# Wk and Wq loaded as fp32 on the sync queue and cast on VectorE and ScalarE; the key constants and the bv centring moved to later places

## The chip, the cores and the metric

The kernel runs as one program on all 8 cores of one Trainium2 chip. Each core computes two of the sixteen sequences and exchanges nothing with the others. The metric is the device time of the slowest core in microseconds, as a median over runs.

## What is computed

One transformer layer over X of 16 sequences, T = 2048 tokens, E = 1024 channels. The attention part, cut to what matters here (the softmax runs over the queries i, axis -2, and there is a residual with a layernorm behind it):

```python
q = einsum('bte,fe->btf', X, Wq) + bq
k = einsum('bte,fe->btf', X, Wk) + bk
v = einsum('bte,fe->btf', X, Wv) + bv
scores = where(j > i, -inf, einsum('bie,bje->bij', q, k) / sqrt(E))
x = layernorm(X + einsum('bij,bje->bie', softmax(scores, axis=-2), v))
```

Behind it stand three feed-forward blocks, each of two 1024 x 1024 linear layers whose weights are dequantized (q/7.5 - 1, times a scale per 16 columns) with a rank-32 addition (lora), a layernorm and a GELU between them, a residual around each block, and a last layernorm.

## The kernel before

**Engines and queues.** The program is written as five in-order lists, one for each engine (`pe`, `dve`, `act`, `pool`, `sp`). Each entry names the tokens it waits for, and it holds up everything behind it on its engine. `pool.dma` issues a transfer on GpSimd's queue, `sp.dma` one on SyncE's. A transfer may change the type only on GpSimd's.

**Order of the work on a core.** The scores need only the product B = Wk^T Wq, so the key and query projections are never formed.

- Constants: `cf` and `cb` are loaded on SyncE. VectorE writes a few memsets, one of them `ones_f` (token `k_of`). Two small fp32 matmuls on TensorE use them, and they are first in TensorE's list.
- BT: 128 matmuls of 128x512 in two halves h of 64 each (8 banks, the contraction index o outermost). The matmuls of o wait for `k_wk[o]` and `k_wq[h][o]`. Behind each half the 8 banks are evicted to bf16 by VectorE and ScalarE in turn.
- Small vectors: 2 x 64 matmuls of 128x2 (`small_vec`).
- `h_chunk` for the four X chunks of 512 tokens: 8 groups of 8 matmuls each, evicted by VectorE and ScalarE in turn. `v_chunk`: 8 groups, each evicted by VectorE with `BVC` (bv with its mean taken off) added, so each waits for `k_bvc`.
- `c_bias`: 32 matmuls of 32x512 that sum over X, then ScalarE copies the bank into `RS` (`tc`) and `SQ` (`th`), and then come 16 one-column fp32 matmuls that turn the row into columns (the key constants, `S_CJ`); every fourth one waits for the one before. The softmax's exponent uses them, the V groups don't.
- Scores and softmax by `s_row`, weighted sums by `pv_chunk`, then the feed-forward part.

In the first sequence the order is h_chunk 0 to 3, centring of Wv after chunk 2, centring of bv, `c_bias`, v_chunk 0 to 3. In the second it is h_chunk 0, then h_chunk and v_chunk in turn, `c_bias`, v_chunk 3; bv is loaded again after h_chunk 0, since its space was used in between.

**Work in the background.** The 48 pieces of dequantization (`dq_slot`) are placed in the lists every 39 units, where a group of 8 matmuls counts 8 units. A slot puts a ScalarE scaling that waits for the load of the integer weights (`qw_t`), a GpSimd product with the scales (`sc_t`), two lora matmuls on TensorE, two VectorE sums, for even layers a ScalarE cast, and the next two 512 KB loads on SyncE. A slot's scaling uses loads that the slot before it issued.

**PSUM.** 8 banks go round in a fixed ring: `bank_take` gives the one returned longest ago. A group whose bank has not been evicted waits.

**Loads at the start.** GpSimd's queue holds 8 loads of Wk rows and 16 of Wq half rows, all cast to bf16 on the way, then three X chunks, the lora parts and the last X chunk, all cast too. SyncE's list holds `cf`, `cb`, then Wv, bv and the first dequantization loads, all behind `k_x[1]`, the second X chunk.

Of the kernel before, what the change touches and what calls it, by code (L numbers as in the profile page):

```python
# [11 lines left out]
AF = mybir.ActivationFunctionType  # L12
# [6 lines left out]
EC = 8  # L19
# [8 lines left out]
A_H = 10240  # L28
A_V = 18432
# [97 lines left out]
def build_program():  # L127
# [4 lines left out]
    wq = din("wq", [E, E], F32)  # L132
    wk = din("wk", [E, E], F32)
    wv_t = din("wv_t", [E, E], F32)
    bv_h = din("bv_h", [128, E], F32)
# [11 lines left out]
    with ExitStack() as ctx:  # L147
# [14 lines left out]
        f32v = lambda a, n: plf[:, a:a + n]  # L162
# [13 lines left out]
        pe, dve, act, pool, sp = (Queue(newsem()) for _ in range(5))  # L176
        slot = lambda: Slot(newsem())
# [4 lines left out]
        def bank_take():  # L182
            return free.pop(0)
# [5 lines left out]
        groups = [0]  # L189
        units = [0.0]  # L190
# [4 lines left out]
        def after_groups(n, fn):  # L195
            due.append((groups[0] + n, fn))
            due.sort(key=lambda d: d[0])
# [35 lines left out]
        def v_stt(out, a, s, b, op0, op1, *after, acc=None, rev=False):  # L233
# [4 lines left out]
        s_cf, s_cb, s_bv = slot(), slot(), slot()  # L238
# [4 lines left out]
        WK = [b16v(A_R + o * 512, 1024) for o in range(EC)]  # L243
        WQ = [b16v(A_DQ + o * 512, 1024) for o in range(EC)]
        XT = [[b16v(A_XT + s * 2048 + c * 256, 512) for c in range(EC)] for s in range(4)]
        XT3 = [b16v(A_XT + s * 2048, 4096).rearrange("p (c t) -> p c t", t=TT)
               for s in range(4)]
        xsrc = [xt[s].rearrange("(c p) t -> p c t", p=128) for s in range(NSEQ)]
        k_wk, k_wq = [None] * EC, [[None] * EC, [None] * EC]
        for o in range(EC):  # L250
            k_wk[o] = pool.dma(slot(), WK[o], wk[o * 128:(o + 1) * 128, :])
            k_wq[0][o] = pool.dma(slot(), WQ[o][:, 0:512], wq[o * 128:(o + 1) * 128, 0:512])
        s_q1 = slot()
        for o in range(EC):
            k_wq[1][o] = pool.dma(slot() if o in (0, EC - 1) else s_q1, WQ[o][:, 512:1024],
                                  wq[o * 128:(o + 1) * 128, 512:1024])
        for o in range(1, EC - 1):
            k_wq[1][o] = (s_q1.sem, s_q1.n)
        s_x = [slot() for _ in range(4)]

        def load_x(seq, ic, s, *after):
            return pool.dma(s_x[s], XT3[s], xsrc[seq][:, :, ic * TT:(ic + 1) * TT], *after)
# [5 lines left out]
        def load_lora(first):  # L268
# [5 lines left out]
            for d in range(2):  # L274
                for dst, src in ((la, la_h[first:first + 2]),
# [2 lines left out]
                                       src.rearrange("w r e -> (w r) e"), *lora_free))  # L278
            k_lora[:] = ks

        k_x = [load_x(0, ic, ic) for ic in range(3)]
        load_lora(0)
        k_x.append(load_x(0, 3, 3))
        k_wv = [sp.dma(slot(), f32v(A_V + o * 1024, 1024), wv_t[o * 128:(o + 1) * 128, :],
                       k_x[1]) for o in range(EC)]
        k_bv = sp.dma(s_bv, f32v(A_BVC, 1024), bv_h, k_x[1])


# [37 lines left out]
        for h in range(2):  # L326
            bk = [bank_take() for _ in range(EC)]
            for o in range(EC):
                for et in range(EC):
# [4 lines left out]
                    if o == EC - 1:  # L334
                        dst, src = BT[et][:, h * 512:(h + 1) * 512], ps[bk[et][0]][:]
                        if et % 2:
                            t = a_act(dst, src, AF.Copy, p)
                        else:
                            t = dve.put(lambda e, d=dst, s=src: e.tensor_copy(d, s), p)
# [34 lines left out]
        BVC = f32v(A_BVC, 1024)  # L374

        def centre_wv():
            for c in range(EC):
                st = f32v(A_V + c * 1024, 1024)
                rs = col(S_ROW + c)
                t = a_act(st, st, AF.Copy, k_wv[c], acc=rs)  # L380
                t2 = v_ts1(col(S_ROW + 8 + c), rs, 1.0 / E, ALU.mult, t)
                k_wvc.append(v_ts1(WV[c], st, col(S_ROW + 8 + c), ALU.subtract, t2))

        def centre_bv(tok):
            t = a_act(BVC, BVC, AF.Copy, tok, acc=col(S_T + 26))
            t2 = v_ts1(col(S_T + 27), col(S_T + 26), 1.0 / E, ALU.mult, t)
            return v_ts1(BVC, BVC, col(S_T + 27), ALU.subtract, t2)
# [106 lines left out]
        sq_free = [None] * NSQ  # L494
# [11 lines left out]
        def h_chunk(seq, jc, xs):  # L506
            for ft in range(EC):
                b, fr = bank_take()
                for c in range(EC):
                    p = mm(ps[b][:], BT[c][:, ft * 128:(ft + 1) * 128], XT[xs][c],  # L510
                           c == 0, c == EC - 1, k_bt[c][ft // 4], k_x[jc],
                           *(fr if c == 0 else ()), sig=c == EC - 1)
                dst = Hb[:, 4 * jc:4 * jc + 4, ft, :]
                src = ps[b][:].rearrange("p (j t) -> p j t", t=128)
                if ft % 2:
                    t = a_act(dst, src, AF.Identity, p, k_u, bias=col(S_U + ft), scale=1.0 / 32)
                else:
                    t = v_ts(dst, src, 1.0 / 32, col(S_U + ft), ALU.mult, ALU.add, p, k_u)
                k_h[jc].append(t)
                p_hlast[0] = p  # L520
                bank_give(b, t)
                group_end(8)
# [16 lines left out]
        def c_bias(seq, slots):  # L539


            b, fr = bank_take()
            b2, fr2 = bank_take()
            for c in range(EC):
                for jc in range(4):
                    g = 32 * jc
                    p = mm(ps[b][g:g + 32, :], hl[:, 32 + 32 * c:64 + 32 * c], XT[slots[jc]][c],
                           c == 0, c == EC - 1, k_w, k_x[jc], *fr, sig=c == EC - 1)
            tc = a_act(RS, ps[b][:], AF.Copy, p, *rs_free)
            th = a_act(SQ[0], ps[b][:], AF.Copy, p, sq_free[0])  # L550
            tl = v_tt(SQ[1], ps[b][:], SQ[0], ALU.subtract, th, tc, sq_free[1])
            bank_give(b, tl)
            for i, tok in enumerate((th, tl)):
                a = 2 * A_SQ + 512 * i
                k_mean[i] = sp.dma(s_mean[i], means[seq, :, i], plb[1:98:32, a:a + 512], tok)
                sq_free[i] = k_mean[i]
            rows = None
            for jt in range(16):
                g = 32 * (jt // 4)
                p = mm(ps[b2][:, jt:jt + 1],  # L560
                       RS[g:g + 1, (jt % 4) * 128:(jt % 4 + 1) * 128],
                       sm[g:g + 1, S_ONE:S_ONE + 1], True, True, tc, k_one, rows, *fr2,
                       sig=jt % 4 == 3)
                if jt % 4 == 3:
                    rows = p
            rs_free[:] = [p]

            t = v_ts(sm[:, S_T + 40:S_T + 56], ps[b2][:, 0:16], float(E), col(S_T + 24),
                     ALU.mult, ALU.add, p, k_bqbk)
            bank_give(b2, t)  # L570
            k_cj[0] = v_ts1(sm[:, S_CJ:S_CJ + 16], sm[:, S_T + 40:S_T + 56], 1.0 / 32, ALU.mult, t)
            groups[0] += 2
            units[0] += 12

        def load_mr(seq, ic):

# [238 lines left out]
        for seq in range(NSEQ):  # L815
            sl = slots[seq]
            k_h = [[] for _ in range(4)]
            k_v = [None] * 16
            if seq == 0:
                for jc in range(4):  # L820
                    h_chunk(seq, jc, sl[jc])
                    if jc == 2:
                        centre_wv()
                k_bvc = centre_bv(k_bv)
                c_bias(seq, sl)
                load_r(0, 0)
                load_r(0, 1)
                for ic in range(4):
                    v_chunk(seq, ic, sl[ic])
            else:  # L830
                for ic in range(4):
                    h_chunk(seq, ic, sl[ic])
                    if ic > 0:
                        v_chunk(seq, ic - 1, sl[ic - 1])
                    if ic == 0:

                        k_bvc = centre_bv(sp.dma(s_bv, BVC, bv_h, *sq_free))
                        load_r(1, 0)
                    if ic == 2:
                        while pieces:  # L840
                            pieces.pop(0)()
                        load_r(1, 1)
                c_bias(seq, sl)
                v_chunk(seq, 3, sl[3])
            k_x_next = [None] * 4
            prev = None
            load_mr(seq, 0)
            load_mr(seq, 1)
            for ic in range(4):
                if ic == 3 and seq == 1:  # L850
                    ffn_prefetch()
                for jt in (range(0, 6), range(6, 10), range(10, 16), ())[ic]:
                    row = s_row(jt, sl)
                    if prev is not None:
                        z_row(prev)
                    prev = row
                    if seq == 0 and jt % 4 == 3:
                        k_x_next[jt // 4] = load_x(1, jt // 4, jt // 4, xt_read[jt // 4])
                if ic == 2:
                    z_row(prev)  # L860
                pv_chunk(seq, ic)
            if seq == 0:
                k_x = k_x_next
# [330 lines left out]
```

How the kernel before makes its waits and increments, by code:

```python
    def emit(self, e, last):  # L108
        for todo, fn, sem, by in self.items:
            for s, v in todo:
                e.wait_ge(s, v)
            inst = fn(e)
            if sem is not None:
                inst.then_inc(sem, by)
        for s, v in last:
            e.wait_ge(s, v)
```

## Time and profile before

| what | value |
|---|---|
| median of 3 runs | 1403.29 us (1401.22 to 1404.46) |
| profiled execution, its own time | 1395.1 us |
| its span on the slowest core (core 2) | 1393.5 us |
| spans of the eight cores | 1381.3 to 1393.5 us |
| TensorE busy, share of the span | 1300.7 us, 93% |
| ScalarE, VectorE, GpSimd busy | 746.1, 704.3, 356.1 us |
| mean granted TensorE clock, by core | 0.975 to 0.981 |
| HBM read, written | 158.85, 46.15 MB |

The profiled execution is 8 us shorter than the median of the unprofiled runs; sums over its rows are made against 1395.1 us and carried over to the median as a difference. Rows name instructions by the tensors they touch: POOLT is the one large SBUF tensor in which X, the weights and all intermediate tiles lie; CF, CB, SM and HL are small constants and statistics; ps are the PSUM banks. A transfer that casts is counted by the bytes that it writes. "Idle before" is the time for which the engine did nothing just ahead of a row, with the event that ended it.

### The profile page before, as it was taken

Reading aid. Unit: us, or ns where it says so; the run is one execution under the profiler, and the core shown is the slowest. Engines: PE = TensorE matmul, PEld = TensorE weight load, DVE = VectorE, ACT = ScalarE, POOL = GpSimd, SP = SyncE. Lnnn points to the kernel's source line nnn. Section 1 sums busy time; section 2 is a strip of 40 time slices with the busy share of each in tenths; the row PEclk is TensorE's granted clock in tenths of the full one; section 3 lists DMA queues with packets and bytes.
Section 4 is the critical chain, followed back from the end, with each engine's and each line's share of the span. In section 5 each row is a group of like instructions: output and inputs, shape, how many; then the busy total and the mean of one; then the engine's idle time right before and its main releaser. Section 6 shows DMA issues by size and latency. Waiting matters only on the chain.

```text
span 1393.5 us, 21058 instructions; the slowest of 8 cores (1381.3 to 1393.5 us)
## 1 busy us (share of the span) xinstructions
PE 1300.7 (93%) x6611; PEld 611.1 (44%) x6740; DVE 704.3 (51%) x1487; ACT 746.1 (54%) x1100; POOL 356.1 (26%) x284
## 2 busy tenths in 40 slices
PE   5997999898899999999999999999899999999994
PEld 2444444443344444444444444455444444444552
DVE  1133556543344456446553483677435534736774
ACT  0153226663223276536855884776578558748641
POOL 5022333565543225332000075001100000840010
PEclk9998999999999999999999999999999999999997
DMA  9956546796856345692101055025801010640032
GB/s 136 208 187 208 178 142 165 216 254 234 295 146 212 114 152 186 216 364 87 61 1 61 1 198 165 0 98 206 287 16 61 1 61 20 207 137 1 31 121 91
DMA packets 71371, 192.61 MB, mean 138 GB/s; under 512 B 6032, under 2 KB 16864, under 8 KB 68192
## 3 DMA queue, kind: packets, MB, share of 16 engines
q1 hardware_dynamic: 48352, 133.45, 29.1%
q0 software_dynamic: 22912, 57.81, 15.2%
q8 instruction: 57, 0.93, 0.3%
q14 instruction: 50, 0.41, 0.1%
HBM read 158.85 MB, written 46.15 MB: 147 GB/s over the span
## 4 chain that ended last, share of the span: by engine, by line
PE 72%; DMA 10%; DVE 6%; issue 4%; ACT 4%; POOL 2%; SPq 1%; DVEq 0%; ACTq 0%; POOLq 0%
PE ps L217 72%; ACT POOLT L221 4%; DMA POOLT<-qw_t 3%; DMA POOLT<-xt 2%; DMA x1s<-POOLT 2%; DVE POOLT L225 2%; DVE SM L1032 1%; POOL POOLT L105 1%; DVE SM L234 1%; DMA POOLT<-bv_h 1%; SPq L105 1%; DMA POOLT<-sc_t 1%; DMA POOLT<-lb_h 1%; POOL POOLT L684 1%; DVEq L111 0%
## 5 line engine op out<-in xcount | busy, mean ns | idle before, releaser
L217 PE MATMUL ps<-POOLT 128*128 128x512 bf16 (+3 forms) x5476 | 1225.2, 375 | 37.1 <-DMA POOLT<-wq 11.5
L217 PEld LDWEIGHTS ps<-POOLT 128*128 128x128 bf16 x5600 | 532.9, 98 | 664.5 <-issue 91.7
L221 ACT ACTIVATE POOLT<-ps,SM 128x512 bf16<-128x512 f32 (+4 forms) x396 | 262.2, 682 | 249.3 <-PE ps L217 152.2
L225 DVE TENSOR_TENSOR POOLT<-POOLT 128x512 bf16<-128x512 bf16 (+1 forms) x448 | 256.4, 608 | 209.5 <-ACT POOLT L221 187.0
L221 ACT ACTIVATE POOLT<-POOLT 128x512 bf16<-128x512 f32 (+4 forms) x234 | 175.3, 762 | 225.1 <-DMA POOLT<-qw_t 108.1
L225 DVE TENSOR_TENSOR POOLT<-ps,POOLT 128x512 bf16<-128x512 f32 (+1 forms) x186 | 124.2, 688 | 151.9 <-PE ps L217 126.9
L990 POOL TENSOR_TENSOR POOLT<-POOLT 128x512 f32<-128x512 f32 x64 | 89.6, 1424 | 371.1 <-DMA POOLT<-x1s 361.9
L411 POOL TENSOR_TENSOR POOLT<-POOLT 128x1024 f32<-128x1024 f32 x48 | 112.7, 2348 | 263.1 <-DMA POOLT<-sc_t 169.6
L221 ACT ACTIVATE POOLT<-POOLT,CF 128x512 bf16<-128x512 bf16 x192 | 154.3, 808 | 27.5 <-DVE POOLT L225 26.5
L221 ACT ACTIVATE POOLT<-POOLT,SM 128x512 bf16<-128x512 f32 (+2 forms) x120 | 109.8, 917 | 83.3 <-DVE SM L228 47.8
L234 DVE SCALAR_TENSOR_TENSOR POOLT<-ps,SM,POOLT 128x512 f32<-128x512 f32 x128 | 96.1, 750 | 80.8 <-PE ps L217 80.3
L217 PE MATMUL ps<-POOLT,CB 128*128 128x512 bf16 (+2 forms) x331 | 96.8, 383 | 24.5 <-ACT POOLT L221 13.4
L684 POOL TENSOR_TENSOR POOLT<-POOLT 128x1024 f32<-128x1024 f32 x32 | 75.0, 2362 | 54.7 <-ACT POOLT L221 53.5
L221 ACT ACT_TABLE_LOAD x48 | 61.6, 1283 | 34.8 <-PE ps L217 30.7
L105 POOL DMA_DIRECT2D out<-POOLT x28 | 15.0, 535 | 252.0 <-ACT POOLT L221 252.0
L600 DVE TENSOR_REDUCE SM<-ps 128x1 f32<-128x512 f32 (+3 forms) x80 | 48.9, 611 | 39.7 <-PE ps L217 36.4
L217 PEld LDWEIGHTS ps<-POOLT,CB 128*128 128x128 bf16 (+2 forms) x336 | 25.6, 96 | 66.0 <-issue 45.8
L228 DVE TENSOR_SCALAR POOLT<-ps,SM 128x512 bf16<-128x512 f32 (+1 forms) x36 | 26.9, 755 | 45.8 <-PE ps L217 45.0
L1032 DVE BATCH_NORM_STATS2 SM<-ps 128x6 f32<-128x512 f32 x64 | 43.4, 692 | 10.9 <-PE ps L217 9.0
L217 PEld LDWEIGHTS ps<-CB,POOLT 128*128 128x128 bf16 x512 | 34.4, 99 | 15.4 <-issue 0.6
L217 PE MATMUL ps<-CB,POOLT 128*128 128x128 bf16 x512 | 39.5, 221 | 0.0
L105 POOL DMA_DIRECT2D weffs<-POOLT x48 | 28.6, 597 | 41.8 <-ACT POOLT L221 33.4
(53 smaller groups left out, 250.7 us busy)
## 6 DMA issues: line engine op xcount, KB each, us to landing
POOLT<-qw_t SPq DMA_DIRECT2D x48, 512.0 KB, 4.0
POOLT<-sc_t SPq DMA_DIRECT2D x48, 512.0 KB, 5.5
POOLT<-weffs SPq DMA_DIRECT2D x24, 1024.0 KB, 7.8
POOLT<-xt SPq DMA_DIRECT2D x16, 1024.0 KB, 10.5
x1s<-POOLT POOLq DMA_DIRECT2D x16, 1024.0 KB, 9.2
POOLT<-x1s SPq DMA_DIRECT2D x8, 2048.0 KB, 11.8
POOLT<-x1s SPq DMA_DIRECT2D x64, 256.0 KB, 3.1
out<-POOLT POOLq DMA_DIRECT2D x28, 512.0 KB, 3.8
```

Source lines behind the costliest of these rows:

```text
L105: self.items.append((todo, lambda e: e.dma_start(out=out, in_=in_), slot.sem, 16))
L217: return pe.put(lambda e: e.matmul(out, lhsT, rhs, start=start, stop=stop), *after, sig=sig)
L221: return act.put(lambda e: e.activation(out, in_, func, bias=bias, scale=scale, accum_out=acc), *after)
L225: return dve.put(lambda e: e.tensor_tensor(out, a, b, op), *after)
L228: return dve.put(lambda e: e.tensor_scalar(out, a, s1, s2, op0, op1), *after)
L234: return dve.put(lambda e: e.scalar_tensor_tensor(out, a, s, b, op0, op1, accum_out=acc, reverse1=rev), *after)
L411: dq_ab[s] = pool.put(lambda e: e.tensor_tensor(q, q, f32v(a + 1024, 1024), ALU.mult), t, dq_ld[s][1])
L600: t = dve.put(lambda e, b=b, lo=lo, n=n: e.tensor_reduce(col(ro + n), ps[b][:, lo:512], AX.X, ALU.max, negate=True), p)
L684: ta = pool.put(lambda e: e.tensor_tensor(r3, r3, rb, ALU.mult), t, *k_r)
L990: tr = pool.put(lambda e, h=h, q=q: e.tensor_tensor(h, h, FXR[q], ALU.add), kx, hb[o], th)
L1032: tb.append(dve.put(lambda e, b=b, k2=k2, fo=fo: e.bn_stats(sm[:, fo + 6 * k2:fo + 6 * k2 + 6], ps[b][:]), p, *fin_free[i]))
```

## The change

Four edits are made together.

1. Wk and Wq are loaded as fp32 on SyncE's queue into staging space (Wk where H will lie, Wq where Wv's staging lies). VectorE casts each Wk block to bf16 (`load_k`), ScalarE each Wq half block (`load_q`).
2. The first three X loads, still on GpSimd's queue with a cast, wait for `q_ld[1][5]`, the load of the 22nd of the 24 weight blocks. Each Wv load waits for the cast that frees its staging space as well.
3. In `c_bias` the 16 one-column matmuls and the two VectorE operations behind them go to a function of their own, `c_columns`, which runs 6 groups later, among the V groups.
4. bv: in the first sequence it is centred behind `c_bias` and not ahead of it. In the second it is loaded at the same place as before, and centred after h_chunk 1 and not after h_chunk 0.

```diff
+        def load_q(h, o):
+            dst = f32v(A_V + o * 1024 + h * 512, 512)
+            q_ld[h][o] = sp.dma(slot(), dst, wq[o * 128:(o + 1) * 128, h * 512:(h + 1) * 512])
+            k_wq[h][o] = act.put(lambda e: e.activation(
+                WQ[o][:, h * 512:(h + 1) * 512], dst, AF.Copy, bias=0.0, scale=1.0), q_ld[h][o])
+
+        def load_k(o):
+            dst = f32v(A_H + o * 1024, 1024)
+            t = sp.dma(slot(), dst, wk[o * 128:(o + 1) * 128, :])
+            k_wk[o] = dve.put(lambda e: e.tensor_copy(WK[o], dst), t)
+
         for o in range(EC):
-            k_wk[o] = pool.dma(slot(), WK[o], wk[o * 128:(o + 1) * 128, :])
-            k_wq[0][o] = pool.dma(slot(), WQ[o][:, 0:512], wq[o * 128:(o + 1) * 128, 0:512])
...
+            load_k(o)
+            load_q(0, o)
         for o in range(EC):
...
+            load_q(1, o)
...
-        k_x = [load_x(0, ic, ic) for ic in range(3)]
+        k_x = [load_x(0, ic, ic, q_ld[1][5]) for ic in range(3)]
...
-                       k_x[1]) for o in range(EC)]
+                       k_x[1], k_wq[1][o]) for o in range(EC)]
...
+            groups[0] += 2
+            units[0] += 12
+            after_groups(6, lambda: c_columns(tc))
+
+        def c_columns(tc):
+            b2, fr2 = bank_take()
             rows = None
             for jt in range(16):
...
+                c_bias(seq, sl)
                 k_bvc = centre_bv(k_bv)
-                c_bias(seq, sl)
...
                 for ic in range(4):
                     h_chunk(seq, ic, sl[ic])
+                    if ic == 1:
+                        k_bvc = centre_bv(k_bv)
                     if ic > 0:
                         v_chunk(seq, ic - 1, sl[ic - 1])
                     if ic == 0:
 
-                        k_bvc = centre_bv(sp.dma(s_bv, BVC, bv_h, *sq_free))
+                        k_bv = sp.dma(s_bv, BVC, bv_h, *sq_free)
                         load_r(1, 0)
```

The head of VectorE's list (the eight casts are those of Wk; L299 writes `ones_f`, for which TensorE's first matmul waits):

```order
-L1139 UNCONDITIONAL_BRANCH
-L289 MEMSET POOLT 128x128
-L290 MEMSET SM 128x1
-L291 MEMSET SM 128x1
-L292 MEMSET HL 128x256
+L1154 UNCONDITIONAL_BRANCH
+L262 CAST POOLT<-POOLT 128x1024 x8
+L299 MEMSET POOLT 128x128
+L300 MEMSET SM 128x1
+L301 MEMSET SM 128x1
+L302 MEMSET HL 128x256
 L231 TENSOR_SCALAR HL<-CF 128x16
```

The casts stand ahead of the memsets, because the list is filled in the order in which the code is written and `load_k` is called first.

TensorE's list around `c_bias` of the first sequence (the 264 are the four h_chunks with 8 lora matmuls, the 32 are `c_bias`, the 16 of one column are the key constants):

```order
 L217 MATMUL ps<-POOLT 128x512 x264
 L217 MATMUL ps<-POOLT,HL 32x512 x32
+L217 MATMUL ps<-POOLT 128x512 x50
 L217 MATMUL ps<-SM,POOLT 128x1 x16
-L217 MATMUL ps<-POOLT 128x512 x278
+L217 MATMUL ps<-POOLT 128x512 x228
```

Six V groups (48 matmuls) and one slot's two lora matmuls now stand between `c_bias` and the columns. The second sequence shows the same move.

ScalarE's list around the second centring of bv (128x4x128 are evictions of h_chunk groups, the plain 128x1024 are the scalings of the dequantization, which wait for `qw_t`; the one that also writes SM is the centring's sum):

```order
 L221 ACTIVATE POOLT<-ps,SM 128x4x128 x2
 L221 ACTIVATE POOLT<-POOLT 128x1024
-L221 ACTIVATE POOLT<-ps,SM 128x4x128
+L221 ACTIVATE POOLT<-ps,SM 128x4x128 x3
+L221 ACTIVATE POOLT<-POOLT 128x1024
+L221 ACTIVATE POOLT<-ps,SM 128x4x128 x2
+L221 ACTIVATE POOLT<-POOLT 128x1024
 L221 ACTIVATE POOLT,SM<-POOLT 128x1024
-L221 ACTIVATE POOLT<-ps,SM 128x4x128 x2
-L221 ACTIVATE POOLT<-POOLT 128x1024
-L221 ACTIVATE POOLT<-ps,SM 128x4x128 x2
-L221 ACTIVATE POOLT<-POOLT 128x1024 x2
```

The centring has moved behind all four evictions that ScalarE makes of h_chunk 1 and behind two more scalings, the second of which stands right ahead of it.

## Rows read from the trace of the kernel before

**Rows 1.** The page: busy times, and the chain that ended last, by engine

```profile
PE 1300.7 (93%) x6611; PEld 611.1 (44%) x6740; DVE 704.3 (51%) x1487; ACT 746.1 (54%) x1100; POOL 356.1 (26%) x284
...
PE 72%; DMA 10%; DVE 6%; issue 4%; ACT 4%; POOL 2%; SPq 1%; DVEq 0%; ACTq 0%; POOLq 0%
```

**Rows 2.** Timeline of TensorE, core 2: start, duration, ..., [idle before, what ended it]

```profile
3.39 0.63 PE L217 MATMUL ps<-CF,POOLT 128*128 128x48 f32 x2 [3.39 <-DMA CF<-cf_h]
9.17 5.83 PE L217 MATMUL ps<-POOLT 128*128 128x512 bf16 x16 [4.67 <-DMA POOLT<-wq]
...
35.85 12.25 PE L217 MATMUL ps<-POOLT 128*128 128x512 bf16 x55 [2.08 <-DMA POOLT<-wq]
51.47 31.30 PE L217 MATMUL ps<-POOLT 128*128 128x512 bf16 x135 [0.19 <-issue]
83.56 23.46 PE L217 MATMUL ps<-POOLT 128*128 128x512 bf16 x106 [0.80 <-ACT POOLT L221]
```

**Rows 3.** Busy time by stretch, core 2; last three: granted clock, DMA share, GB/s

```profile
10.00:15.00 5.00, 4.99 (x15) 1.65 (x13) 0.00 (x0) 0.00 (x0) 5.00 (x10) 1.00 1.05 129
...
30.00:35.00 5.00, 3.16 (x14) 1.06 (x11) 2.18 (x4) 3.24 (x5) 0.00 (x0) 1.00 1.17 172
...
50.00:55.00 5.00, 4.81 (x62) 2.57 (x60) 0.76 (x4) 0.00 (x0) 0.00 (x0) 0.66 1.11 171
...
70.00:75.00 5.00, 4.95 (x24) 2.25 (x23) 0.75 (x1) 0.69 (x1) 0.00 (x0) 1.00 1.01 302
```

**Rows 4.** Waits of SyncE's queue: total us, times, longest

```profile
SPq L111 <- DMA POOLT<-xt: 47.9, 1, 47.9
```

**Rows 5.** Timeline of VectorE at the start, and its casts by shape

```profile
1.16 0.17 DVE L289 MEMSET POOLT<- 128x128 f32 x1 [1.16 <-PEq L128]
3.71 0.08 DVE L298 DVE_READ_ACCUMULATOR SM<-CF 128x1 f32 x1
...
L764 DVE CAST POOLT<-POOLT 128x2048 bf16<-128x2048 f32 x8 | 9.4, 1220 | 0.0
```

**Rows 6.** Timeline around c_bias of the first sequence

```profile
112.48 1.91 PE L217 MATMUL ps<-POOLT,HL 128*32 128x512 bf16 x32
115.48 1.06 ACT L221 ACTIVATE POOLT<-POOLT 128x1024 f32<-128x1024 int32 x1 [3.81 <-DMA POOLT<-qw_t]
119.08 1.07 ACT L221 ACTIVATE POOLT<-ps 128x512 f32<-128x512 f32 x2
119.81 7.77 PE L217 MATMUL ps<-SM,POOLT 1*128 1x1 f32 x32 [5.42 <-ACT POOLT L221]
127.91 13.55 PE L217 MATMUL ps<-POOLT 128*128 128x512 bf16 x51 [0.33 <-issue]
```

**Rows 7.** Busy time by stretch behind that c_bias, columns as in Rows 3

```profile
118.00:120.00 2.00, 0.19 (x1) 0.22 (x2) 0.61 (x2) 2.00 (x5) 2.00 (x2) 0.87 0.60 145
...
132.00:134.00 2.00, 2.00 (x8) 0.83 (x7) 1.34 (x5) 0.41 (x1) 0.00 (x0) 0.71 1.00 316
```

**Rows 8.** Timeline and one stretch around the second bv load

```profile
369.51 1.06 ACT L221 ACTIVATE POOLT<-POOLT 128x1024 f32<-128x1024 f32 x1 [11.18 <-DMA POOLT<-bv_h]
...
372.78 12.48 PE L217 MATMUL ps<-POOLT 128*128 128x512 bf16 x50 [4.44 <-DVE POOLT L228]
...
374.00:376.00 2.00, 2.00 (x7) 0.78 (x6) 1.15 (x2) 0.00 (x0) 1.86 (x2) 0.63 1.01 415
```

**Rows 9.** Timeline and one stretch around c_bias of the second sequence

```profile
455.11 2.19 PE L217 MATMUL ps<-SM,POOLT 1*128 1x1 f32 x16 [1.26 <-ACT POOLT L221]
457.44 3.81 PE L217 MATMUL ps<-SM,POOLT 1*128 1x1 f32 x16
461.59 17.65 PE L217 MATMUL ps<-POOLT 128*128 128x512 bf16 x74 [0.33 <-issue]
...
464.00:466.00 2.00, 2.00 (x10) 0.91 (x9) 0.69 (x1) 0.00 (x0) 0.00 (x0) 0.94 0.00 0
```

**Rows 10.** The same columns on core 6, timeline

```profile
455.36 4.77 PE L217 MATMUL ps<-SM,POOLT 1*128 1x1 f32 x32 [1.26 <-ACT POOLT L221]
```

More of the change, by code:

```diff
@@ L249, in build_program @@
         k_wk, k_wq = [None] * EC, [[None] * EC, [None] * EC]
+        q_ld = [[None] * EC, [None] * EC]
+        def load_q(h, o):
[7 more added lines that the diff above has]
+            k_wk[o] = dve.put(lambda e: e.tensor_copy(WK[o], dst), t)
         for o in range(EC):
-            k_wk[o] = pool.dma(slot(), WK[o], wk[o * 128:(o + 1) * 128, :])
-            k_wq[0][o] = pool.dma(slot(), WQ[o][:, 0:512], wq[o * 128:(o + 1) * 128, 0:512])
-        s_q1 = slot()
+            load_k(o)
+            load_q(0, o)
         for o in range(EC):
[L255 to L258, printed above, removed]
+            load_q(1, o)
         s_x = [slot() for _ in range(4)]
@@ L542, in c_bias @@
             b, fr = bank_take()
-            b2, fr2 = bank_take()
             for c in range(EC):
@@ L571, in c_bias @@
             k_cj[0] = v_ts1(sm[:, S_CJ:S_CJ + 16], sm[:, S_T + 40:S_T + 56], 1.0 / 32, ALU.mult, t)
-            groups[0] += 2
-            units[0] += 12
         def load_mr(seq, ic):
```

## The prediction

> **What bounds the kernel now.** I read the page first: TensorE is busy for 93% of the span and makes 72% of the chain that ended last [rows 1]. So an edit is worth what it takes from TensorE's list: gaps, work, or time at the lower clock. I then went through the timeline of TensorE alone for gaps, and looked only at the three places that the change touches. At the start TensorE waits for weights: its first large group begins at 9.17, the last wait of this kind ends at 35.85, and the H groups begin at 51.47 [rows 2]. Around the first `c_bias` it stands idle for 5.42 us, then runs the one-column matmuls for 7.77 us, then goes on at half clock [rows 6, 7]. Around the second bv load it stands for 4.44 us [rows 8], and around the second `c_bias` for 1.26 us [rows 9]. Everything behind moves with TensorE, so I add up these four places on core 2, the slowest.
>
> **The start: a loss.** Before, TensorE needs only Wk[0] and half of Wq[0] to begin, and works on while the rest lands. Now its very first matmul waits for `ones_f`, and VectorE writes that behind all eight casts of Wk. So the BT stage can't begin until Wk[7] has landed, although by then nearly all other weights are there. What is queued behind this wait is TensorE's whole list.
>
> When does Wk[7] land? Ahead of it, itself included, stand eight Wk blocks of 0.524 MB and seven half blocks of 0.262 MB: 6.03 MB. The first transfer (cf) ended TensorE's wait at 3.39 [rows 2]. For the rate I take 302 GB/s, the stretch in which fp32 loads of 4 KB rows from SyncE's queue ran with the transfer engines full [rows 3]: 6.03/0.302 = 20.0 us, so 23.4 us. Half blocks queued behind will get some share, since the sixteen engines don't run in step; an estimate of 1.5 us puts it at about 25 us. The bounds of the rate are the casting loads of before, counted by their fp32 source: 129 GB/s written is 258 read, 172 is 344 [rows 3]. They give 26.8 and 20.9 us, and with the same allowance at most 28.5.
>
> From there, step by step. The cast of 128x1024: the row of twice the size takes 1.22 us [rows 5]; less an assumed fixed 0.15 us, half of it is 0.7. Then VectorE's small operations: from 1.16 to 3.79, less the wait for cf inside, 1.0 us [rows 5], and the second small matmul 0.55; the old wait for Wq began at 9.17 - 4.67 = 4.50, which fits [rows 2]. BT begins near 27.3. Its 128 matmuls, now without a wait: 56 took 12.25 us (one record is missing), 0.219 each, so 28.0. The first 16 took 5.83 and not 3.5, as the clock starts low, 2.3 more [rows 2]. I add 0.2 for the banks between the halves: 30.5 us, ending near 57.8. The second halves of Wq, 8.39 MB in all, are there by 3.4 + 27.8 = 31 and needed from 42 on; ScalarE's sixteen casts end by 33, ahead of its first eviction. Then the small vectors: 51.47 - (35.85 + 12.25) = 3.4 us. The H groups begin at 61.2 and not at 51.47: **a loss of 9.7 us**, 5.6 to 13.2 by the bounds.
>
> The X loads wait behind the weights, but the first is cast and landed well before 61: from 29 us on, 2.1 MB of source at these rates is 7 us. SyncE was held until about 50 by the second X chunk (47.9 us of wait [rows 4]); that chunk now lands at about the same time, so Wv and the first dequantization loads do too. TensorE comes 9.7 us later to them, so the 0.80 us gap before 83.56 [rows 2], where ScalarE waited for `qw_t` with evictions behind it, should go: **0.8 us gained**. GpSimd loses 24 issues ahead of X; nothing waits for them.
>
> A rule of the Trainium skill speaks against hoping for more from the new queue: "DMA: Bandwidth & Descriptors", section "Issuing engines are not separate DMA queues", says that transfers issued by any engine run on the same 16 engines, and that another issuer saves only issue time. By it the weights land no sooner than the bytes allow; the rows agree (DMA share 1.05 to 1.17 with GpSimd's queue [rows 3]).
>
> **The first c_bias.** Its matmuls end at 112.48 + 1.91 = 114.39. ScalarE stood for `qw_t` until 115.48 and had a last H eviction and bv's centring to do before the two copies at 119.08. The columns ran from 119.81, and V began at 127.91: 13.5 us [rows 6]. The clock row of 0.87 puts the fall to the lower level at 119.5, and the row of 0.71 the rise at 133.2 [rows 7]. V thus ran 5.25 us at half speed and lost 2.6. Together **16.1 us**. Now V follows `c_bias` at once. Its evictions wait for `k_bvc`, some 2.5 us behind the copies, near 121.5 on the old time. By then three or four V groups, `c_bias` and the last H group hold banks of the ring of eight, so TensorE doesn't stop. The columns remain as work. At the full clock they take 4.77 us [rows 10]; on core 2 the clock fell within them (2.19 us for the first half, 3.81 for the second [rows 9]). Bounds: 4.8 with nothing behind, and 7.77 + 0.33 + 2.6 = 10.7 when all is as slow as before. Now busy V groups stand ahead of them and no idle stretch, so I take a value near the fast end: 4.8 + 0.3, and 1.3 for a fall that comes late, 6.4. **Gain 9.7 us** (5.4 to 11.3).
>
> The skill's page "TensorE: Matmul & The Clock Gate", section "What's actually happening", says that the throttled clock is the default and that activity releases it. By this the columns, which keep the array nearly empty, still bring a fall; with the full slow price the sum would be 4.3 us worse at each place.
>
> **The second c_bias.** It ends at 455.11 - 1.26 = 453.85 and V begins at 461.59: 7.7 us. The row of 0.94 puts the clock's rise at 464.2 [rows 9], so V lost 1.3 more: 9.0 us. Less the same 6.4: **gain 2.6 us** (-1.7 to 4.2).
>
> **The second bv.** ScalarE waited 11.18 us for bv, with H evictions behind it, and TensorE 4.44 us for a bank. The row of 0.63 puts the clock's rise at 375.5, so 2.7 us from 372.78 at half speed cost 1.35 more [rows 8]. Now bv, which landed at 369.5, is asked for after h_chunk 1, near 372. **Gain 5.8 us** (0 if a new wait takes its place, see below).
>
> **Sum.** 9.7 + 2.6 + 5.8 + 0.8 = 18.9 gained, 9.7 lost: 9.2 us less, 1395.1 to 1385.9 for the profiled execution. The median of the runs shown is 1403.3, so 1394.1.
>
> **Rivals.**
>
> Loads faster than I take. At 344 GB/s without drift Wk[7] lands at 20.9, the start costs 5.6 and the net is -13.3; with the columns at their fast end at both places -16.5, so 1387 to 1390. For it speaks the 172 row; against it that it stood in one stretch only. The skill's first page above, section "Anatomy of one DMA", fits 436 GB/s behind a fixed 2 us; by that Wk[7] would land near 17 and the net would be -17. The one row above 400 GB/s is a stretch of 2 us (415 [rows 8]); stretches of 5 us stay at 302 or below, by fp32 source at 344.
>
> The gap by bv returns elsewhere. A scaling that waits for `qw_t` now stands right ahead of the centring [the order above shows it]. Its load is issued when bv and two X halves are under way, and TensorE is there 5.8 us earlier. If it lands 8 us or more behind h_chunk 1, V groups fill the ring of banks and TensorE stops again: up to 5.8 us come back. That alone makes the net -3.4; slow columns at both places alone (8.6 us) make it -0.6; both +5.2. So 1400, 1403 or 1408.5. Against it: eight banks are a cover of some 12 us of V groups.
>
> The start swallows it all, and the kernel is slower. The mechanism is the gate on Wk[7] alone: if the transfer engines serve the 24 weight blocks side by side, Wk[7] lands when all 8.39 MB have: at 302 GB/s at 31.2, a loss of 15.9 and a net of -3.0; at 258 GB/s at 35.9, a loss of 20.6 and a net of +1.7. It decides from 34 us on; from 37 us on the kernel is slower by over 0.2%, 1407 us or so. For it speaks that the half blocks are short rows; against it, that one queue serves its transfers roughly in the order of issue.
>
> That the change does nothing is hard to hold: the gate on `ones_f` and the moved columns are both in the lists.
>
> **Chances and range.** My forecast, net -5 to -13, 1390 to 1398: 0.50. Faster loads: 0.14. A gap that returns or slow columns: 0.18. A start that swallows most or all: 0.18, half of it beyond zero net. 1386 to 1404 leaves out the ends of the last two. A measurement of this kernel tells 0.2%, some 2.8 us, from no change. Faster by over 0.2%: 0.74 (the first two, and a little over half of the third). Within 0.2%: 0.14. Slower: 0.12 (the start beyond 37 us, or both parts of the third).
>
> **What would show it.** In the profile after: the one wait of TensorE at the start ended by VectorE's memset near 26 us and BT without gaps behind; H groups from about 61; no idle time between `c_bias` and V in either sequence; the columns as one row of 5 to 6 us among V groups; no 4 us gap near 370. I am wrong if H begins past 70, if a wait on bank evictions shows in the V groups, or if the clock is low for over 4 us around the columns.

## The result, and the profile after

The change makes the kernel slower: 1408.66 us in the median of six runs against 1403.55 of the kernel before, a ratio of 1.0038 [1.002, 1.0056], some 5.3 us. The profiled execution took 1409.76 us. Its span is that of core 6 (1408.2), and cores 4 to 7 have a lower granted clock in it (0.968 to 0.971) than cores 0 to 3 (0.976 to 0.982), which those of before didn't show. So I read the change on core 2, which the prediction used: 1393.5 before, 1398.0 after. Executions in which some cores ran long stretches at a lower granted clock are left out of every ratio and mean core, but for one experiment where I say so; the medians in us beside them are taken over all executions.

The page, slowest core: busy times and the chain that ended last, as in [rows 1].

```profile
PE 1307.5 (93%) x6611; PEld 609.7 (43%) x6740; DVE 711.2 (51%) x1495; ACT 758.3 (54%) x1116; POOL 342.3 (24%) x260
...
PE 77%; DMA 7%; DVE 6%; issue 4%; ACT 3%; SPq 1%; POOL 1%; DVEq 0%; ACTq 0%; POOLq 0%
```

VectorE has 8 more instructions and ScalarE 16 (the casts), GpSimd 24 fewer (the issues). The share of waits for transfers in the chain fell from 10% to 7% [rows 1], and the kernel is slower all the same.

TensorE's timeline at the start, core 2, to be held against [rows 2]:

```profile
26.90 0.63 PE L217 MATMUL ps<-CF,POOLT 128*128 128x48 f32 x2 [26.90 <-DVE SM L301]
27.59 0.56 PE L217 MATMUL ps<-SM,POOLT 128*128 128x1 f32 x2
28.01 30.68 PE L217 MATMUL ps<-POOLT 128*128 128x512 bf16 x128
58.53 3.39 PE L217 MATMUL ps<-HL,POOLT 128*128 128x2 bf16 x128
61.78 3.40 PE L217 MATMUL ps<-POOLT 128*128 128x512 bf16 x9
```

VectorE's, with the first and the last of the eight casts of Wk, and two stretches of 5 us (granted clock, DMA share, GB/s at the end):

```profile
7.95 0.69 DVE L262 CAST POOLT<-POOLT 128x1024 bf16<-128x1024 f32 x1 [7.95 <-DMA POOLT<-wk]
...
25.92 0.69 DVE L262 CAST POOLT<-POOLT 128x1024 bf16<-128x1024 f32 x1 [1.26 <-DMA POOLT<-wk]
26.59 0.17 DVE L299 MEMSET POOLT<- 128x128 f32 x1
```

```profile
10.00:15.00 5.00, 0.00 (x0) 0.00 (x0) 1.07 (x2) 1.44 (x3) 0.00 (x0) 1.00 0.95 287
15.00:20.00 5.00, 0.00 (x0) 0.00 (x0) 1.70 (x3) 1.68 (x3) 0.00 (x0) 1.00 1.03 343
```

There is one wait of 26.9 us where there were several: `ones_f` is written at 26.59, behind the cast of Wk[7], and TensorE's first matmul follows it. Then the BT stage runs without a gap. Its first matmuls start 0.43 us apart and those behind 34 us 0.216, as at the start of BT before (16 matmuls in 5.83 us [rows 2]). The granted clock says 1.00 in both stretches all the same, so at the very start that column doesn't show what TensorE ran at:

```profile
28.00:32.00 4.00, 4.00 (x11) 1.47 (x12) 1.40 (x8) 2.53 (x5) 0.00 (x0) 1.00 0.94 320
36.00:40.00 4.00, 4.00 (x20) 1.85 (x19) 0.00 (x0) 0.00 (x0) 3.03 (x6) 1.00 1.01 115
```

Around the first `c_bias`, TensorE, core 2, and four stretches:

```profile
121.78 1.91 PE L217 MATMUL ps<-POOLT,HL 128*32 128x512 bf16 x32
123.62 10.96 PE L217 MATMUL ps<-POOLT 128*128 128x512 bf16 x50
134.51 1.05 PE L217 MATMUL ps<-SM,POOLT 1*128 1x1 f32 x8
135.71 2.19 PE L217 MATMUL ps<-SM,POOLT 1*128 1x1 f32 x16
...
138.59 0.47 PE L217 MATMUL ps<-SM,POOLT 1*128 1x1 f32 x3
138.99 21.28 PE L217 MATMUL ps<-POOLT 128*128 128x512 bf16 x90
```

```profile
139.00:140.00 1.00, 1.00 (x5) 0.45 (x5) 0.72 (x3) 0.00 (x0) 0.00 (x0) 0.77 0.90 348
140.00:142.00 2.00, 2.00 (x6) 0.71 (x5) 1.20 (x5) 0.00 (x0) 0.00 (x0) 0.50 1.04 339
142.00:144.00 2.00, 2.00 (x9) 0.81 (x8) 0.69 (x1) 0.00 (x0) 0.00 (x0) 0.76 0.98 341
144.00:146.00 2.00, 2.00 (x11) 0.91 (x10) 0.69 (x1) 0.00 (x0) 0.00 (x0) 1.00 1.09 335
```

V now follows at once; the 5.42 us of idle time of [rows 6] are gone. The columns take 4.55 us (134.51 to 139.06) and run at the full clock, but the clock falls to its lower level behind them, at 139.5, and rises at 143.0: 3.4 us of V groups at half speed, 1.7 us lost. In the second sequence the clock falls within the columns:

```profile
455.26 1.91 PE L217 MATMUL ps<-POOLT,HL 128*32 128x512 bf16 x32
457.10 10.96 PE L217 MATMUL ps<-POOLT 128*128 128x512 bf16 x50
467.99 5.93 PE L217 MATMUL ps<-SM,POOLT 1*128 1x1 f32 x32
473.86 7.54 PE L217 MATMUL ps<-POOLT 128*128 128x512 bf16 x26
```

Around the second bv, one view after the other: the timelines of TensorE, SyncE's queue, ScalarE and VectorE, and two stretches, all of core 2.

```profile
364.70 21.52 PE L217 MATMUL ps<-POOLT 128*128 128x512 bf16 x99
390.35 27.73 PE L217 MATMUL ps<-POOLT 128*128 128x512 bf16 x116 [4.13 <-DVE POOLT L225]
```

```profile
361.69 0.33 SPq L105 DMA_DIRECT2D POOLT<-bv_h  x1
362.11 1.32 SPq L105 DMA_DIRECT2D POOLT<-xt  x2
369.59 0.34 SPq L105 DMA_DIRECT2D POOLT<-qw_t  x1
```

```profile
375.10 0.69 ACT L221 ACTIVATE POOLT<-ps,SM 128x512 bf16<-128x512 f32 x1 [2.77 <-PE ps L217]
385.13 2.00 ACT L221 ACTIVATE POOLT<-POOLT 128x1024 f32<-128x1024 int32 x2 [9.35 <-DMA POOLT<-qw_t]
```

```profile
387.59 1.81 DVE L231 TENSOR_SCALAR POOLT<-POOLT,SM 128x1024 f32<-128x1024 f32 x1
389.51 5.47 DVE L225 TENSOR_TENSOR POOLT<-ps,POOLT 128x512 bf16<-128x512 f32 x9
```

```profile
390.00:392.00 2.00, 1.65 (x4) 0.59 (x5) 2.00 (x5) 0.00 (x0) 1.91 (x1) 0.50 0.34 131
392.00:394.00 2.00, 2.00 (x6) 0.76 (x5) 2.00 (x4) 0.00 (x0) 0.00 (x0) 0.50 0.00 0
```

The gap of [rows 8] near 370 is gone, and another stands at 386.2 to 390.35, in the V groups. ScalarE waited 9.35 us for `qw_t`; the second of the two activations grouped in the row at 385.13 is bv's centring. The load was issued at 369.59, behind bv and two X halves of 1 MB, and landed at 385.1, 15.5 us later. V's evictions (L225) wait for the centring (L231 ends it), so all eight banks were full, and behind the gap the clock is at its lower level. All eight cores show this gap, 3.93 to 7.86 us long and 5.6 in the mean; before, six cores had one of 2.38 to 4.44 near 370, and the mean over all eight was 2.8.

The first of each kind of operation, read from the traces as a mean over the eight cores, gives the balance by stage (after less before, us; a minus is earlier):

| up to | after | loads alone | columns alone | bv alone |
|---|---|---|---|---|
| first H eviction | +10.3 | +9.8 | -0.2 | +0.7 |
| last H eviction | +8.8 | +8.2 | +0.3 | +0.9 |
| first score row | +1.3 | +8.8 | -7.1 | +0.8 |
| H of sequence 2 begins | +2.2 | +8.3 | -8.6 | -1.3 |
| its third chunk | +5.8 | +8.1 | -9.3 | +1.2 |
| score rows of sequence 2 | +3.9 | +7.9 | -10.7 | +1.8 |
| end | +10.8 | +8.1 | -8.7 | +2.3 |

Over cores 0 to 3 alone the changed kernel ends at +4.7; what cores 4 to 7 lose behind the last score rows is taken up in the last section. Single stages between these points differ by 1 to 2 us from trace to trace.

### The profile page after: what moved, and what is told of

It is laid out like the page before. It is cut to its first block, busy times and chain, and to the rows that moved or that the text cites. A ratio compares the mean times of both kernels' runs of the same rounds, so it can differ in the third digit from the quotient of the medians.

```text
span 1408.2 us, 21109 instructions; the slowest of 8 cores (1388.6 to 1408.2 us)
## 1 busy us (share of the span) xinstructions
PE 1307.5 (93%) x6611; PEld 609.7 (43%) x6740; DVE 711.2 (51%) x1495; ACT 758.3 (54%) x1116; POOL 342.3 (24%) x260
## 4 chain that ended last, share of the span: by engine, by line
PE 77%; DMA 7%; DVE 6%; issue 4%; ACT 3%; SPq 1%; POOL 1%; DVEq 0%; ACTq 0%; POOLq 0%
PE ps L217 77%; ACT POOLT L221 3%; DMA x1s<-POOLT 3%; DMA POOLT<-qw_t 2%; DVE POOLT L225 2%; DVE SM L1047 1%; DMA POOLT<-wk 1%; DVE SM L234 1%; SPq L105 1%; DMA POOLT<-sc_t 1%; DMA POOLT<-lb_h 1%; DVE POOLT L231 1%; POOL POOLT L697 1%; DVEq L111 0%; DVE SM L225 0%
## 5 line engine op out<-in xcount | busy, mean ns | idle before, releaser
L225 DVE TENSOR_TENSOR POOLT<-POOLT 128x512 bf16<-128x512 bf16 (+1 forms) x448 | 255.8, 606 | 214.4 <-ACT POOLT L221 191.2
L225 DVE TENSOR_TENSOR POOLT<-ps,POOLT 128x512 bf16<-128x512 f32 (+1 forms) x186 | 123.1, 687 | 149.8 <-PE ps L217 114.9
L217 PEld LDWEIGHTS ps<-CB,POOLT 128*128 128x128 bf16 x512 | 34.0, 98 | 15.1
L234 DVE SCALAR_TENSOR_TENSOR POOLT<-POOLT,ps 128x512 f32<-128x512 f32 x48 | 30.9, 681 | 12.6 <-POOL POOLT L421 8.6
## 6 DMA issues: line engine op xcount, KB each, us to landing
POOLT<-x1s SPq DMA_DIRECT2D x8, 2048.0 KB, 12.8
```

The lines of the kernel that those rows point to most:

```text
L217: return pe.put(lambda e: e.matmul(out, lhsT, rhs, start=start, stop=stop), *after, sig=sig)
L225: return dve.put(lambda e: e.tensor_tensor(out, a, b, op), *after)
L234: return dve.put(lambda e: e.scalar_tensor_tensor(out, a, s, b, op0, op1, accum_out=acc, reverse1=rev), *after)
```

## The experiments

Each comparison is with the kernel before on the same chip. "Mean core" is the mean of the eight cores' spans over the executions that are compared, less the same of the kernel before.

### The loads alone

The kernel before with edits 1 and 2 only (the first two pieces of the diff).

> The kernel before with the new loads alone (Wk and Wq as fp32 on SyncE's queue, casts on VectorE and ScalarE, X behind them); columns and bv as before. My theory (the gate on Wk[7] costs what the sum said, and nothing gives it back): the H groups begin some 9 to 10 us later than in the kernel before, as they do in the changed kernel (65.1 against 54.8 on core 2), the gap around c_bias stays, and the total is 8 to 11 us over the kernel before. Rival (later waits for loads absorb the delay): H late by 9 to 10 us, but the total within 3 us of the kernel before.

Measured: 1410.03 against 1398.68 us, ratio 1.0067 [1.0042, 1.0091]; mean core +10.0. The first matmul of core 2 starts at 26.86 and H at 61.34. The loads are the loss, of the size forecast, and nothing gives it back: by the table it is 9.8 us at the first H eviction and still 8.1 at the end.

### The columns alone

Edit 3 only.

> The kernel before with the key constants turned six groups behind, and nothing else. Theory: the first gap goes, V follows c_bias at once, some 9 us gained by the first score row on core 2, 1 to 2 us more in the second sequence: 7 to 11 us faster in total. Rival (the gain is taken back by waits for transfers in the first sequence's weighted sums, as 3 to 4 us went there in the changed kernel): 4 to 7 us faster, with the loss between the first and the last weighted sum of the first sequence.

Measured: 1393.03 us, ratio 0.994 [0.9915, 0.9965]; mean core -8.4. Of this 7.1 us come by the first score row, and the weighted sums take nothing back, as the rival had it.

### The second centring alone

Edit 4 in the second sequence only:

```diff
                     h_chunk(seq, ic, sl[ic])
+                    if ic == 1:
+                        k_bvc = centre_bv(k_bv)
...
-                        k_bvc = centre_bv(sp.dma(s_bv, BVC, bv_h, *sq_free))
+                        k_bv = sp.dma(s_bv, BVC, bv_h, *sq_free)
```

> The kernel before with bv of the second sequence centred after h_chunk 1, and nothing else. Theory (a scaling that waits for its integer weights stands ahead of the centring, and that load comes late behind other transfers): a gap of 3 to 5 us returns among the first V groups, total within 2 us of the kernel before. Rival (the forecast): no gap near 370, 4 to 6 us faster.

Measured: 1399.63 us, ratio 1.0 [0.9985, 1.0016]; mean core +2.7. TensorE's timeline, and how long the `qw_t` loads between 340 and 390 took from issue to landing, core 2:

```profile
388.80 13.45 PE L217 MATMUL ps<-POOLT 128*128 128x512 bf16 x54 [5.54 <-DVE POOLT L225]
```

```profile
DMA to landing us min/median/max: 4.8/6.9/16.9
```

The new gap is there without the other edits. It costs all that the old one did, and 2.7 us more in the mean core. By mean cores the three sum to 10.0 - 8.4 + 2.7 = +4.3, and the changed kernel, run again below, has +4.8: there is no large interaction. Edit 4 in the first sequence has no run of its own; it is only in the runs that combine edits.

### Centring ahead of the scaling instead

The kernel before with bv loaded at its place and centred seven groups into h_chunk 1 (`late_centre` does what `k_bvc = centre_bv(k_bv)` did), so that no scaling with a late load stands right ahead of it:

```diff
-                        k_bvc = centre_bv(sp.dma(s_bv, BVC, bv_h, *sq_free))
+                        k_bv = sp.dma(s_bv, BVC, bv_h, *sq_free)
+                        after_groups(7, late_centre)
```

> The kernel before with bv of the second sequence centred after 7 of the 8 groups of h_chunk 1: one group earlier than in the change, so that in ScalarE's list it stands ahead of the scaling that waits for its weights. Theory (the scaling ahead of it made the new gap): no gap of over 1 us in h_chunk 1 or the V groups behind it, 3 to 6 us faster than the kernel before by the third H chunk of the second sequence. Rival (bv itself, or the ring of banks, is what is late, and any later place gives a gap): a gap stays, and the total is within 2 us of the kernel before.

Measured: 1393.16 against 1397.19 us, ratio 0.9945 [0.9922, 0.9968]; mean core -4.4. On core 2 that `qw_t` load is as late as before (16.1 us) and ScalarE waits 9.98 us for it, but neither the centring nor an eviction stands behind it; TensorE has one unbroken row, and no core has a gap of over 1 us there:

```profile
342.07 68.17 PE L217 MATMUL ps<-POOLT 128*128 128x512 bf16 x308
```

### The X halves later

Why did that `qw_t` load take 17 us, when the three before it took 4.8 to 6.9? The run with the bv edit alone, and the two X halves of sequence 2 issued behind v_chunk 0:

```diff
                         k_bv = sp.dma(s_bv, BVC, bv_h, *sq_free)
+                    if ic == 1:
                         load_r(1, 0)
```

> The kernel before with the second bv centred after h_chunk 1, and the two X halves of load_r(1, 0) issued behind v_chunk 0 and not behind bv. Theory (the qw_t load that the scaling waits for is late, because 2 MB of X halves stand in the transfer engines ahead of it): it lands some 7 us sooner than the 17 us of the run with the bv edit alone, TensorE's gap of 5.54 us near 388 goes or falls under 1 us, and the kernel comes out 3 to 6 us faster than before, ratio 0.996 to 0.998. Rival (the stores of x1s alone make it late, or a centring that simply stands too far back): gap of 3 us or more remains, ratio 0.999 to 1.003.

Measured: 1392.11 against 1397.87 us, ratio 0.9965 [0.995, 0.998]; mean core -3.3. The same two views as for the bv edit alone:

```profile
359.76 42.45 PE L217 MATMUL ps<-POOLT 128*128 128x512 bf16 x196
```

```profile
DMA to landing us min/median/max: 3.8/4.7/6.0
```

The centring stands where the change put it, the longest landing fell from 16.9 to 6.0 us, and the gap is gone on all eight cores. So the lateness came from the 2 MB of X ahead of the load, and with it out of the way the forecast gain of edit 4 is real. By the Trainium skill, "DMA: Bandwidth & Descriptors", section "Issuing engines are not separate DMA queues", transfers of all issuers run on the same 16 engines. The two runs don't test that, since bv, X and `qw_t` are all issued by SyncE: they show that a load is late by what the same issuer has under way ahead of it. GpSimd's stores are in both.

### The gate on Wk[7] taken away

The changed kernel with the memsets and the two small matmuls written ahead of the loads, so that they stand ahead of the casts in VectorE's list (the memset of `ones_f` stands here for the block that moves):

```diff
+        k_of = dve.put(lambda e: e.memset(ones_f, 1.0 / E))
...
         k_wk, k_wq = [None] * EC, [[None] * EC, [None] * EC]
...
-        k_of = dve.put(lambda e: e.memset(ones_f, 1.0 / E))
```

> The changed kernel with the block of small constants (memsets and what hangs on them) written ahead of the loads, so that VectorE does it before the eight casts and TensorE's first matmul waits for no cast. Theory: BT begins near 9 us, H near 47 and not 65; but ScalarE then comes early to the first scaling, whose integer weights land near 80, so that TensorE stops there for 4 to 6 us; in total 8 to 13 us faster than the changed kernel, which is 3 to 8 us faster than the kernel before. Rival (the weights on SyncE's queue land no earlier, block by block, than on GpSimd's): H near 52, and the total 8 us faster than the changed kernel.

Measured: 1392.63 against 1398.68 us, ratio 0.9954 [0.9937, 0.9972]; mean core -3.7. ScalarE's and TensorE's timeline, core 2:

```profile
30.13 4.46 ACT L291 ACTIVATE POOLT<-POOLT 128x512 bf16<-128x512 f32 x7 [1.12 <-DMA POOLT<-wq]
34.50 2.04 ACT L221 ACTIVATE POOLT<-ps 128x512 bf16<-128x512 f32 x4
```

```profile
12.13 13.07 PE L217 MATMUL ps<-POOLT 128*128 128x512 bf16 x48 [7.74 <-ACT POOLT L291]
...
35.22 16.70 PE L217 MATMUL ps<-POOLT 128*128 128x512 bf16 x63 [5.14 <-ACT POOLT L221]
```

In the mean core this is 8.5 us faster than the changed kernel (+4.8, run again below), the low end of what I expected and just as well the rival's 8; the places are neither's. BT begins at 12.13 on core 2 and not at 9.17: Wq[0] lands at 10.06, and ScalarE's table load (1.28 us) and cast (0.63) follow. On that block the rival is right: SyncE's queue brings it no sooner than GpSimd's did. H (after the row at 35.22 and the small vectors) begins only at 55, and so the stop expected near 80 doesn't come. The cast load has a second price, which the gate had hidden: ScalarE's casts of Wq's second halves stand ahead of its four evictions of BT's first half, and TensorE waits 5.14 us for them, then runs on at the lower clock (0.50 in the stretch from 35 to 40).

### Both mended, and a version that keeps the old loads

Two combinations. The first keeps the fp32 loads, with the gate taken away, the casts of Wq's second halves placed behind the first half's evictions and shared by VectorE and ScalarE, Wv's loads written behind them, and bv centred as seven groups into h_chunk 1. The second keeps the old loads and has the columns six groups behind, the first centring behind `c_bias`, and the same centring of the second bv.

> The same with the new loads kept, but mended twice: the small constants are done ahead of the casts, and the casts of Wq's second halves stand behind the evictions of the first BT half, four on each of VectorE and ScalarE. Theory (the new queue brings the weights no sooner; all that the loads cost was order in the lists): H begins at 50 to 52, level with the kernel before, and the total is within 2 us of the kernel with the old loads and the other two edits. Rival (loads on SyncE's queue cost by themselves, by X that comes later): 4 us or more slower than that kernel.

> The changed kernel with the old loads (cast on GpSimd's queue) and with the second bv centred one group earlier: columns six groups behind, bv of the first sequence behind c_bias. Theory: the gains of the columns (8.4) and of the bv place (3 to 6) add up, 11 to 14 us faster than the kernel before. Rival (waits for transfers take back what TensorE gains earlier): 6 to 10 us faster.

Measured on one chip, before 1397.19 us. Mended loads: 1398.95 us (1389.4 over the three executions compared), ratio 0.9932 [0.9907, 0.9957], mean core -8.0. Old loads: 1384.96 us, ratio 0.9902 [0.9879, 0.9924], mean core -11.2, over three as well, where the single edits sum to -8.4 - 4.4 = -12.8. With mended loads the first H eviction comes 1.4 us earlier than before in the mean over the cores, and the last 4.5 us later (old loads: 0.8 later both). On core 2 TensorE stands in the H stage behind a scaling, and SyncE comes to Wv, with the dequantization loads behind it, at 52.39, where it came at 49.90 in the kernel before (second row), since it waits for the second X chunk:

```profile
85.36 25.96 PE L217 MATMUL ps<-POOLT 128*128 128x512 bf16 x106 [4.56 <-ACT POOLT L221]
```

```profile
52.39 4.35 SPq L105 DMA_DIRECT2D POOLT<-wv_t  x8
```

```profile
49.90 4.97 SPq L105 DMA_DIRECT2D POOLT<-wv_t  x8
```

So here too the fp32 loads are worth nothing: what the start gains, the wait for `qw_t` takes, in part because TensorE is there earlier and in part because X, and with it `qw_t`, lands later, which is the rival's mechanism. The difference between the two lies between my "within 2 us" and the rival's "4 us or more" (3.2 us in the mean core, 4.5 between the medians of the executions compared), and their intervals overlap.

### The best version again, with and without the later X halves

> The same program as the fastest so far, for the comparison on one chip: 11 to 14 us faster than before, ratio 0.990 to 0.992.

> The fastest version so far (old loads, columns six groups behind, bv centred a chunk part ahead) with the same later X halves. Theory: bv and the scalings have no gap there any more, so the later load has nothing to give: within 1.5 us of the same version without it on this chip. Rival (the crowd of transfers also costs elsewhere): 2 us or more faster.

Measured, before 1397.87 us: 1382.82, ratio 0.9903 [0.9885, 0.9921], and with the later X halves 1382.29, ratio 0.9901 [0.9884, 0.9918]. The version beats the kernel before by 1% on both chips, and the changed kernel by more, and the X halves matter only while a scaling that V waits for stands behind them.

### The changed kernel again

> The changed kernel again, on the chip of the other experiments. Theory (the edits add up: loads +10, columns -8.4, the second bv +2.7 in the mean over the cores): 3 to 6 us slower than the kernel before, as far on one die as on the other. Rival (something of the whole change, not of its parts, costs more, as the 10 us by which cores 4 to 7 were behind in its profile): 8 us slower or more.

Measured: 1417.88 against 1397.19 us, ratio 1.01 [1.0059, 1.0141]. This ratio isn't one of the edits alone: in four of the seven executions that are compared, at least one pair of cores had a lower mean granted clock (about 0.96), and these took 1415.1 to 1420.9 us. The three without it took 1401.5 to 1403.5, some 5 us over the kernel before, mean core +4.8, as expected. Such a pair stands in 8 of all 11 executions of the changed kernel and in none of the 16 of the kernel before on this chip, but also in one of 5 and two of 6 of the two combinations. So the change may well bring it on; which edit does isn't settled. See the last section.

## Why the prediction was wrong

I forecast -9.2 us, and +5.3 was measured. Two of the three signs that I had named for being wrong came true: a wait on evictions in the V groups, and in the second sequence a clock that was low for over 4 us around the columns (6.8 us, from about 470.6 to 477.4). By the steps of the prediction:

- **The start: a loss of 9.7.** Right. BT began at 28.0 on core 2 (forecast 27.3), H at 61.8 (61.2), the first H eviction 10.3 us late on core 2 and in the mean; with the loads alone it is 9.8 in the mean. The rate of 302 GB/s that I took lies between those of the two stretches (287 and 343). The rivals "loads faster" and "the start swallows it all" are out: the casts show the weights landing in order, Wk[7] at 25.9. The 436 GB/s that the prediction took from the Trainium skill is a fit for transfers that GpSimd issues; these are SyncE's, and no stretch of 5 us of them moved more than 343.
- **0.8 us in the H stage.** Right in kind; up to the last H eviction 1.5 us came back.
- **The first `c_bias`: gain 9.7.** Right on core 2: from the first matmul of `c_bias` to the first score row 10.0 us less, with 6.25 us for the columns (4.55, and 1.7 at the lower clock) against 6.4. But the mean core gained 7.5. I had summed on the slowest core, and a core that stands longest at one place isn't the one that sets the end after it is mended.
- **The second `c_bias`: gain 2.6.** Oversized by half. 1.3 by the rows: 5.93 us of columns, and V at the lower clock until about 477.4, in all 7.7 against the 6.4 of the sum; over the mean core the stage gained 1.9. The Trainium skill's page "TensorE: Matmul & The Clock Gate", section "What's actually happening", by which the clock is low unless activity releases it, had spoken for this: even between dense groups the clock fell at the columns, behind them in the first sequence (3.4 us low) and within them in the second (6.8 us).
- **The second bv: "Gain 5.8 us". This is the step that failed.** It cost 3.6 us in the changed kernel (from the first H group of sequence 2 to its third chunk) and +2.7 in the mean core alone. The rival "the gap by bv returns elsewhere" had the mechanism, the place and its condition: `qw_t` lands 8 us or more behind h_chunk 1. It landed 10 us behind (on core 2 the last group of h_chunk 1 ends at 375.1, the load lands at 385.1). I gave it too little weight on the word that "eight banks are a cover of some 12 us". The cover was sized right: V groups filled the banks from about 375 to 386.2, 11 us. The need wasn't worked out. It is the landing, then scaling, centring and first eviction, 5.2 us (385.13 to 390.35), so 15 in all; and the load's own time, 15.5 us behind bv and X, could have been bounded from [rows 8], where bv alone kept ScalarE waiting for 11.18. I also priced the return at up to 5.8 us, back to zero. It costs more than the old gap did: it averages 5.6 us over the cores against 2.8, and the clock is down behind it. With the centring placed elsewhere, or X loaded later, the step gives 4.4 and 3.3 us in the mean core; that is what it was worth, and the 5.8 were too much even so, since core 2 had the longest of the old gaps (4.44).

The balance: forecast, on core 2, 9.7 - 0.8 - 9.7 - 2.6 - 5.8 = -9.2; measured, in the mean over the cores up to the score rows of sequence 2, 10.3 - 1.5 - 7.5 + 3.6 - 1.9 = +3.0, and +0.9 in the weighted sums of sequence 1, so +3.9. The bv step is 9.4 of the miss, the first `c_bias` 2.2, and the rest lies in small terms. That the changed kernel's profile ends at +10.8 and not near +4 isn't the edits' directly but a lower clock on some cores, shown in the last section; the executions run again without it have +4.8.

## What to carry to other kernels

When a waiting instruction is moved back, look at what stands right ahead of it at its new place in the in-order list, and ask when that one's own load lands, counted behind every transfer then under way; an accumulator ring covers only the few microseconds that its groups take. A load that is split into transfer and cast can pay twice more, in what the casts delay on their engines: here the constants behind the casts, then the evictions. And sum a change over the cores' mean, not on the core that waits longest at the place in question.

## What the hardware showed that I had not expected

Loads of 512 KB land in 3.8 to 6.0 us when little is ahead of them, and in 15.5 to 16.9 with bv, 2 MB of X and stores under way (`qw_t` on core 2, with X moved away and with X ahead). And the granted clock has a third level, 0.81, beside 1.00 and 0.50. In one execution of the changed kernel run again, cores 2 and 3 stood at it for some 150 us, TensorE busy, while core 0 had 1.00. The stretch from 200 to 220, core 3 first, then core 0:

```profile
200.00:220.00 20.00, 20.00 (x93) 9.10 (x93) 10.32 (x23) 7.45 (x18) 3.50 (x3) 0.81 0.40 133
```

```profile
200.00:220.00 20.00, 20.00 (x107) 9.41 (x106) 13.00 (x34) 13.13 (x30) 6.82 (x6) 1.00 0.57 158
```

Core 3 made 93 matmuls where core 0 made 107. It comes in pairs of neighbouring cores, and the executions with it are some 12 to 19 us longer than those without.

The profile of the changed kernel itself has it too, and this is what cores 4 to 7 lost behind the last score rows. The same stretch on core 6, and then on core 0:

```profile
630.00:638.00 8.00, 7.91 (x31) 3.26 (x30) 6.57 (x4) 2.06 (x3) 7.44 (x5) 0.81 0.84 334
```

```profile
630.00:638.00 8.00, 6.10 (x28) 2.62 (x27) 7.30 (x6) 2.06 (x3) 6.67 (x5) 1.00 0.62 248
```

Added up over that trace, cores 6 and 7 stand at 0.81 for 74 us in 12 spells, 4 and 5 for some 61 in 9, 2 and 3 for 15 in one, 0 and 1 never. That takes 14, 11, 3 and 0 us of clock. Behind the score rows of sequence 2 these pairs of cores lost 12.2 and 15.1, 11.3 and 10.6, 2.3 and 4.9, and -0.2 and -1.1 us against the kernel before, whose profile has the level on no core. No run here tells what brings it on.
